# Routed experts of a transformer block: page row numbers copied out, an expert converted every third page, token sums kept by lanes, and the last two pages added on TensorE

## The reference

```
x = x + ln(attention(ln(x)))            # 16 heads of 16, RoPE, causal
t = ln(x)                               # 2048 x 256
combine = top-4 of softmax(t @ gate_w.T), 16 experts, renormalised
shared  = (silu(t@Wg) * (t@Wu)) @ Wd * sigmoid(t @ gate_vec)       # 704 wide
sparse  = sum over experts e of combine[:, e] * ((silu(t@Ge)*(t@Ue)) @ De)   # 176 wide
x = x + ln(shared + sparse)
```

## Time and profile before

| | |
|---|---|
| median of 3 executions | 587.03 us |
| lowest, highest | 582.26, 588.21 us |
| profiled execution, own time | 591.91 us |
| its span in the profile | 590.2 us |
| busy: TensorE, VectorE, ScalarE, GpSimd | 523.0, 412.6, 344.1, 317.2 us |
| page loop and what follows | from about 396 us to the end |

### The profile page before, as it was taken

One profiled execution on the slowest core, in us unless ns is written; L12 is line 12 of the kernel. 1 busy time (PEld: TensorE's weight loads), 2 busy tenths in 40 slices (PEclk: granted clock), 3 DMA queues, 4 the chain that ended last, 5 costly groups with the idle time before them and its releaser, 6 DMA issues.

```text
span 590.2 us, 11696 instructions
## 1 busy us (share of the span) xinstructions
PE 523.0 (89%) x3590; PEld 400.3 (68%) x3590; DVE 412.6 (70%) x1019; ACT 344.1 (58%) x704; POOL 317.2 (54%) x341
## 2 busy tenths in 40 slices
PE   8978889899999998879879887879989899999964
PEld 3744454656565453458668776769988899999953
DVE  4888878898788856688634552557977666566846
ACT  3443665686578558766443324547876766666633
POOL 4822724481465225222766656405758777778662
PEclk9988999999999999989899989799999999999987
DMA  8543560734073440520235412558999887788975
GB/s 310 159 120 116 186 205 4 217 113 140 27 222 109 141 142 3 170 83 2 85 131 184 165 72 98 185 160 200 223 209 235 146 138 133 129 146 174 280 174 204
DMA packets 71659, 87.66 MB, mean 149 GB/s; under 512 B 6640, under 2 KB 64560, under 8 KB 71600
## 3 DMA queue, kind: packets, MB, share of 16 engines
q1 hardware_dynamic: 56720, 67.22, 36.6%
q0 software_dynamic: 14448, 19.31, 18.0%
q10 hardware_dynamic: 432, 0.39, 0.2%
HBM read 34.99 MB, written 39.12 MB: 126 GB/s over the span
## 4 chain that ended last, share of the span: by engine, by line
PE 27%; DMA 7%; DVE 6%; issue 5%; another core or an unknown queue 4%; POOL 3%; ACT 3%; SPq 1%; POOLq 0%; ACTq 0%; DVEq 0%
PE gate_ps L2150 9%; PE y_ps L2173 5%; DMA acc_dram<-yout,xin 5%; PE y_ps L2124 2%; PE gate_ps L1092 2%; PE m_ps L2073 2%; PE up_ps L1092 2%; POOL acc_dram L1595 1%; DMA added<-acc_dram 1%; DVE hid_lo L1881 1%; PE up_ps L2161 1%; PE y_ps L2177 1%; DVE hid L1853 1%; PE up_ps L2162 1%
## 5 line engine op out<-in xcount | busy, mean ns | idle before, releaser
L1595 POOL DMA_INDIRECT acc_dram<-yout,xin x79 | 124.8, 1580 | 60.5 <-DMA acc_dram<-yout,xin 22.9
L815 DVE TENSOR_REDUCE nmax<-a_ps 128x2 f32<-128x768 f32 (+3 forms) x88 | 96.3, 1121 | 16.0 <-PE a_ps L983 15.5
L678 ACT ACTIVATE probs<-a_ps 128x1024 f32<-128x1024 f32 (+1 forms) x96 | 81.6, 883 | 30.9 <-PE a_ps L1008 26.3
L570 POOL TENSOR_SCALAR_AFFINE_SELECT probs<-probs 128x256 f32<-128x256 f32 (+1 forms) x96 | 47.2, 501 | 87.4 <-ACT probs L678 87.2
L1583 POOL DMA_INDIRECT xs_dram<-xrow,idx x64 | 66.5, 1040 | 37.3 <-issue 18.6
L2150 PE MATMUL gate_ps<-w_all,rxT_hi 128*128 x316 | 77.4, 327 | 3.8 <-DVE rxT_lo L1929 2.4
L1954 DVE TENSOR_TENSOR h<-rsilu,gate_ps 128x176 f32<-128x176 f32 x79 | 26.6, 336 | 45.1 <-ACT rsilu L1705 40.3
L2173 PE MATMUL y_ps<-w_all,hT_hi 128*128 x237 | 57.2, 310 | 1.0 <-DVE hT_lo L1966 0.7
L978 PE MATMUL a_ps<-KTt,QT 96*128 96x128 bf16 (+3 forms) x256 | 50.8, 309 | 5.7 <-ACT probs L678 1.8
L2150 PEld LDWEIGHTS gate_ps<-w_all,rxT_hi 128*128 128x128 f32 x316 | 51.8, 188 | 5.5 <-issue 5.0
L1008 PE MATMUL a_ps<-QT,KTt 99*128 99x512 bf16 (+3 forms) x256 | 47.9, 301 | 4.7 <-DVE nmax L815 1.7
(11 more groups left out here) (341 smaller groups left out, 1388.2 us busy)
## 6 DMA issues: line engine op xcount, KB each, us to landing
xin<-xs_dram SPq DMA_DIRECT2D x79, 136.5 KB
xs_dram<-zeros SPq DMA_DIRECT2D x7, 1365.0 KB, 6.5
w_all<-in_wex_dram SPq DMA_DIRECT2D x16, 480.0 KB
KTt<-parts SPq DMA_DIRECT2D x42, 128.0 KB
QT<-parts SPq DMA_DIRECT2D x39, 128.0 KB
acc_dram<-zeros SPq DMA_DIRECT2D x6, 640.0 KB, 7.7
ring<-acc_dram SPq DMA_DIRECT2D x18, 128.0 KB
acc_dram<-yst SPq DMA_DIRECT2D x4, 512.0 KB
```

The lines of the kernel that those rows point to most:

```text
L570: pool.affine_select(out=pr, in_=pr, pattern=[[0, nh], [1, P]], compare_op=ALU.is_ge, fill=0.0, base=0, channel_multiplier=-1).then_inc(ma ...
L678: nc.scalar.activation(dst, src, ACT.Exp, scale=float(DH) ** -0.5).then_inc(a_act, 1)
L815: nc.vector.tensor_reduce(nmax[:, i, h:h + nh].rearrange("p (b h) -> p b h", h=hb), src, AX.X, ALU.max, negate=True).then_inc(a_dve, 1)
L1595: pool.indirect_dma_start(out=acc[a][:, :], out_offset=bass.IndirectOffsetOnAxis(ap=xin[:, p % XIN, XROW - 1:XROW].bitcast(mybir.dt.uint32 ...
```

## The change

Four things are changed; the pages' computation is not.

- Row numbers: `select` copies the row numbers of its two pages out of `xin` into `row_of`, and the scatter takes them from there. A page load then waits until TensorE has turned the page that was in its slot and `select` has read it, no longer for that page's scatter.
- Experts: the conversion of an expert takes every third page instead of every second, in SyncE's order as in ScalarE's and VectorE's: an expert's transfers stand behind the loads of pages 16, 19, 22 and so on. The nine early tiles' loads stand behind all page loads.
- Lanes: `acc` has token row p * 16 + n instead of n * 128 + p (through the table `ids`), so a load of several tiles reads one contiguous run from each lane.
- The last two pages (77 and 78) are not scattered. VectorE builds for each a 128 x 512 matrix of ones and zeros: whether the row of the page (partition) belongs to the token of tiles 12 to 15 (column). TensorE multiplies with it (`spared`, 2 x 4 matmuls) ahead of the sums of tiles 12 to 15; their table comes with one more 256 KB transfer, `lanes`. The order of the three sums is now 2, 0, 1. (One semaphore of `gathered` is replaced by a common one.)

```diff
+SPARED = 2
+        def over_pages(q):
+            c = q % XIN
+            flat = xin[:, c:c + 2, :].rearrange("p a b -> p (a b)")
+            return flat[:, 0:TB * P]
+        lanes, owners = over_pages(67), [over_pages(69), over_pages(72)]
+        def by_lanes(rows):
+            return rows[0:NT * P, :].rearrange("(p n) d -> p n d", n=NT)
...
             def load_page(q):
                 if q >= XIN:
-                    sp.wait_ge(y_added[(q - XIN) % ACCS], 16 * ((q - XIN) // ACCS + 1))
+                    sp.wait_ge(r_turned, q - XIN + 1)
+                    sp.wait_ge(r_sel, (q - XIN) // 2 + 1)
...
-                    sp.dma_start(fetched(i, a), acc[a][i * P:(i + 1) * P, :]).then_inc(early_in[i % RING], 16)
+                    sp.dma_start(fetched(i, a), by_lanes(acc[a])[:, i, :]).then_inc(early_in[i % RING], 16)
...
                 load_page(q)
-                k = early + TAILS + (q - SPLIT - XIN) // 2
-                if q >= SPLIT + XIN and (q - SPLIT) % 2 == 0 and k < E:
+                k, part = divmod(q - SPLIT - XIN, 3)
+                k += early + TAILS
+                if k >= early + TAILS and part == 0 and k < E:
                     expert(k)
-                if FINAL + XIN <= q < FINAL + XIN + RING:
-                    load_early(q - FINAL - XIN)
+            for a in range(ACCS):
+                sp.wait_ge(y_added[a], 16 * len(range(a, FINAL + 1, ACCS)))
+            for i in range(RING):
+                load_early(i)
+            sp.wait_ge(r_turned, 69)
+            sp.wait_ge(r_sel, 35)
+            sp.dma_start(lanes, lanes_in).then_inc(lanes_in_sem, 16)
...
-            for a in (1, 2, 0):
-                sp.wait_ge(y_added[a], 16 * len(range(a, PAGES, ACCS)))
+            for a in (2, 0, 1):
+                sp.wait_ge(y_added[a], 16 * len(range(a, PAGES - SPARED, ACCS)))
                 load_rest(a, PARTS[1], total_in[a])
...
-            for p in range(PAGES):
+            for p in range(PAGES - SPARED):
...
-                        ap=xin[:, p % XIN, XROW - 1:XROW].bitcast(mybir.dt.uint32), axis=0),
+                        ap=row_of[:, p:p + 1].bitcast(mybir.dt.uint32), axis=0),
...
-                k = early + (p - SPLIT - 2) // 2
-                if p >= SPLIT + 2 and k < E:
-                    if (p - SPLIT) % 2 == 0:
+                k, part = divmod(p - SPLIT - 2, 3)
+                k += early
+                if early <= k < E:
+                    if part == 0:
                         expert_high(k)
-                    else:
+                    elif part == 1:
                         expert_tail_high(k)
...
+                nc.vector.tensor_copy(row_of[:, 2 * m:2 * m + n].bitcast(mybir.dt.int32),
+                                      xin[:, at:at + n, XROW - 1].bitcast(mybir.dt.int32))
...
+            def owns():
+                dve.wait_ge(lanes_in_sem, 16)
+                for k in range(SPARED):
+                    q = PAGES - SPARED + k
+                    ins = nc.vector.tensor_copy(named[:, k:k + 1], xin[:, q % XIN, XROW - 1:XROW].bitcast(mybir.dt.int32))
+                link(ins)
+                for k in range(SPARED):
+                    ins = nc.vector.tensor_scalar(owners[k], lanes, named[:, k:k + 1], None, ALU.is_equal)
+                ins.then_inc(owned, 1)
...
+            owns()
             gathered(0)
...
+            def spared():
+                pe.wait_ge(r_y, PAGES)
+                pe.wait_ge(owned, 1)
+                for k in range(SPARED):
+                    for i in range(PARTS[1].start, PARTS[1].stop):
+                        n = i - PARTS[1].start
+                        nc.tensor.matmul(pe_places[i], owners[k][:, n * P:(n + 1) * P],
+                                         yout[:, (PAGES - SPARED + k) % YOUT, :],
+                                         start=k == 0 and n % 2 == 0, stop=False, skip_group_check=True)
...
                 ins.then_inc(pe_summed, 1)
-            pe.wait_ge(r_y, PAGES)
-            for a in (1, 2, 0):
+                if i == 7:
+                    spared()
+            for a in (2, 0, 1):
                 pe.wait_ge(total_in[a], 16)
...
-    ids = np.arange((NT + 1) * P, dtype=np.int32).reshape(NT + 1, P).T
+    ids = np.concatenate([np.arange(NT * P).reshape(P, NT), NT * P + np.arange(P)[:, None]], axis=1)
```

More of the change, by code:

```diff
@@ L1256, in first_slots, with ffn_block @@
     yield
-def ffn_block(nc, t, wsh_in, wex_in, out):
+def ffn_block(nc, t, wsh_in, wex_in, lanes_in, out):
     with ExitStack() as ctx:
@@ L1480, in store_shared @@
                 b = ORDER_S[i]
-                sp.dma_start(acc[0][b * S:(b + 1) * S, :].rearrange("(n p) d -> p n d", p=P),
+                sp.dma_start(by_lanes(acc[0])[:, b * TB:(b + 1) * TB, :],
                              yst[:, i % 2]).then_inc(ysh_stored[i % 2], 16)
@@ L1535, in load_rest @@
                 to = added[:, a - 1] if a else total
-                sp.dma_start(to[:, tiles, :], acc[a][tiles.start * P:tiles.stop * P, :].rearrange(
-                    "(n p) d -> p n d", p=P)).then_inc(landed, 16)
+                sp.dma_start(to[:, tiles, :], by_lanes(acc[a])[:, tiles, :]).then_inc(landed, 16)
             for a in range(ACCS):
                 load_rest(a, slice(EARLY, PARTS[0].stop), rest_in)
-            for a in (1, 2, 0):
-                sp.wait_ge(y_added[a], 16 * len(range(a, PAGES, ACCS)))
+            for a in (2, 0, 1):
+                sp.wait_ge(y_added[a], 16 * len(range(a, PAGES - SPARED, ACCS)))
                 load_rest(a, PARTS[1], total_in[a])
@@ L1969, in _ @@
                     select(p // 2)
-                k = early + (p - SPLIT - 3) // 2
-                if p >= SPLIT + 3 and k < E:
-                    if (p - SPLIT) % 2 == 1:
+                k, part = divmod(p - SPLIT - 3, 3)
+                k += early
+                if early <= k < E:
+                    if part == 0:
                         expert_low(k)
-                    else:
+                    elif part == 1:
                         expert_tail_low(k)
@@ L2237, in build @@
         attention_block(nc, t, x, wqkv, wpair, wo, gw, rope, ids, wsh, cst, cst16)
-        ffn_block(nc, t, wsh, wex, out)
+        ffn_block(nc, t, wsh, wex, lanes, out)
 def kernel(L0_attn_x, L0_attn_Wq, L0_attn_Wk, L0_attn_Wv, L0_attn_Wo, L0_ffn_gate_w, L0_ffn_expert_gate_up,
```

26 lines of the change are left out of this document (15 added, 11 removed).

## The result

| | before | changed |
|---|---|---|
| median of 20 executions each | 588.62 us | 582.05 us |
| lowest, highest | 581.15, 594.43 us | 574.22, 590.86 us |
| ratio, with its 95% interval | | 0.9877 (0.9843 to 0.9910) |
| profiled execution, its span | 591.91, 590.2 us | 582.78, 581.0 us |

The change makes the kernel 1.2% faster, some 7.2 us. The three executions shown before had a median of 587.03 us; 0.9877 times that is 579.8 us, the time forecast. In another series on another chip the same kernel stood at 0.9912 (0.9881 to 0.9943), so the gain is about 0.9% to 1.2%; the medians of all executions stand at 0.9888 and 0.9875. The ratios leave out executions more than 1.5% above the fastest of their kernel, and the profiled execution of the kernel before is one of those.

A forecast was written before the change was run, and what follows sets the result against it. TensorE was taken to bound the calm page loop, with 8.7 us lost where experts are converted. From the median 587.03, 4.6 for the loop and 2.6 for the end gave 579.8 us; range 574 to 588.

The forecast's parts named there:

- The loop's mechanism: Page loop: ScalarE waits 7.8 us for expert transfers queued behind page loads that wait for scatters; freeing these removes it.
- transfers saturated: Rival, expert stretch: the transfers' engines, not queue order, make experts late; only the end gains, 584.4 us; chance 0.12.
- The loop's size: Page loop: 7.0 us saved in the profiled execution (bounds 0 to 8.7), 4.6 us taken for the median.
- pages 0 to 78 in 156 to 158 us: Sign that the forecast is right: the page loop shortened to this from 163.9 us.
- My check for VectorE: Page loop with experts every third page: VectorE needs 5.1 of 5.97 us in three pages, so it has room.
- its 2.6 for the end: Behind the last page: tile 11 done at 573.3 instead of 575.96 us; gain 2.6 us, bounds -2 to +3.
- Copies and `owns` at no cost: VectorE: 40 copies, at most 7.2 us busy, covered by room in the pages; `owns`, 1.9 us, hidden; cost 0.
- Early tiles at zero: Early tiles' loads in one burst behind page 62's landing: bounds -0.9 to +1.5 us, taken as 0.
- under 5: Sign that the forecast is right: loads of three tiles behind the loop take less than 5 us.
- it looks like the end's bound and hardly is: End: the last scatter and its `acc[0]` load seem to bound it, but VectorE waits only 0.22 us for the result.
- without the idle 4.93 us it should keep the full clock: End, TensorE: condition for the spared pages' matmuls costing 3.7 us; at the slow clock they cost 8.3 us.
- The slower rival: Page loop: scatters become the bound from a 6.3 us cycle of three on; 592.8 or 600.8 us; chance 0.12.

The follow-up runs named there:

- u1: Changed kernel with experts converted every second page again instead of every third; 0.9824 of the kernel before.
- e1: Kernel before with only row numbers copied, page loads freed from waiting for scatters, and early tiles' loads behind all page loads; 0.9946 of the kernel before.
- e2: Kernel before with only the conversion of experts moved to every third page; 0.9958 of the kernel before.
- b_again: The kernel before, unchanged, run and profiled a second time; 1.0032 of the kernel before, 0.9995 by the medians.
- u2: Changed kernel with page loads waiting for scatters again, experts still every third page; 1.0028 of the kernel before.
- u4: Changed kernel with the sums' rows back in the old layout by tiles; 0.9863 of the kernel before.
- e3: Kernel before with only the sums' row layout changed to lanes; 1.0026 of the kernel before, 0.9994 by the medians.
- u3: Changed kernel with all 79 pages scattered, none spared, and the last sums in the old order; 0.9947 of the kernel before.
- c_changed: The changed kernel itself, run again in a later series on another chip; 0.9912 of the kernel before.
- s_spared_alone: Kernel before with only the last two pages added by TensorE, plus the row-number copies this needs; 0.9994 of the kernel before, 0.9953 by the medians.
- v1: Changed kernel with experts every second page, measured a second time on another chip; 0.9922 of the kernel before.
- v2: Changed kernel with experts every second page and rows by tiles, leaving only freed page loads and spared pages; 0.9873 of the kernel before.

## Why the prediction was right, and where only its sum was

**The loop's mechanism: right.** ScalarE stood for experts whose fetch stood behind page loads that stood for scatters. With the page loads freed (u1, e1) that wait fell from 7.8 us to 0 and 0.2. The rival "transfers saturated" falls: the share rose to 0.98 and nobody waited. What I hadn't said: the change holds two cures for one wait. Either alone does it (e1: 161.9 us, e2: 160.1 us), and together they bring the loop to 159.4, within the spread of these numbers over kernels with freed loads (158.6 to 161.9 us).

**The loop's size: the term was too large for the profile, right for the median.** I took 7.0 us off the profiled execution and 4.6 off the median, between 2.1 and 7.0 for not knowing which part of the stalls the median execution had. The loop measured 4.5 us shorter in the first pair of profiles and 5.4 against b_again. So the sign "pages 0 to 78 in 156 to 158 us" was missed by 1.4. The other loss remained: 159.4 - 155.2 = 4.2 us, 2.7 of them between pages 6 and 38 and 1.4 from page 68 on. My check for VectorE was a mean, 5.1 of 5.97 us in three pages; on the one step where `select` and the low part meet, VectorE holds TensorE up all the same, but that is 0.5 us in all and the rest of the 2.7 is open. That the sum came out as 579.8 to the tenth is luck: its 4.6 is the middle between two readings of one long execution, its 2.6 for the end turned out 3.3 against one profile of before and nothing against the other, and by the later series it would be 587.03 x 0.9912 = 581.9 us.

**Copies and `owns` at no cost: right.** 40 copies took 8.7 us, 218 ns as the view counts them against the 181 taken; `owns` took 1.2 us, not 1.9; TensorE's spared matmuls 3.62 us for 16 records against 3.7, at full clock.

**Early tiles at zero: right here, by a condition that I didn't name.** u2 shows 8.3 us of standing once page loads wait for scatters. I had weighed the burst and not the place in the queue. e1's 3.0 us show that the cover is thin even with freed loads.

**The end: the number came out, its reasons didn't all.** Tile 11 was done at 567.1 us, 8.9 behind the loop's end, forecast 9.4, before 12.0. But in b_again, with the old kernel, it was done after 8.4 us: the 12.0 belonged to one long execution, and the chain through the load of tiles 9 to 11, from which I took the 2.6 us, is not what the change shortened. That load was there 6.8 us behind its issue, forecast 6.2, so not "under 5"; of the 2.5 us that I allowed for the layout nothing is shown (u4, e3), and b_again has the same end as the changed kernel.

The step "it looks like the end's bound and hardly is" was true of the kernel before and false of the kernel that the other parts make. In every kernel with a stall-free loop and all pages scattered (u3, e1, e2), VectorE stood 3.4 to 4.0 us for the last sum, and the end took 26.5 to 28.4 us. What the spared pages do is keep 2 to 5 us from being given back at the end (c_changed beside e1 and e2, u4 beside u3), and the rows show two halves of it: in u3, e1 and e2 the sums of tiles 12 to 15 start 1.8 to 3.1 us later than in b_again, and 16 of their records take 1.7 to 2.7 us longer, at the lower clock. With them, TensorE has matmuls in the stretch in which it otherwise stands, the first sum is asked for some 6 us sooner than in u3, and the clock stays up. I had named "without the idle 4.93 us it should keep the full clock" as a condition of the cost of 3.7 us; I didn't count it as a gain.

The two profiles of before go the same way: the short end, 22.95 us, is the one at 1.00, the long one, 26.3, the one at 0.58 (its tiles 9 to 11 also landed 2.2 us later). Whether the parts gain more together than singly isn't shown: e1 and s_spared_alone gained 0.5% and 0.1%, v1 and v2, which hold both parts, 0.8% and 1.3%; by the medians it is 0.7% and 0.5% against 1.25% and 1.3%, a plain sum.

**The slower rival: not seen.** It needed a scatter cycle of 6.3 us in the calm stretch. There it was 5.75 us (changed) and 6.10 (e3) against 6.11 (b_again 6.10), and beside experts 7.08 against 7.14. (Its 592.8 and 600.8 us were counted from 168.0 us for 79 pages; 79 x 163.9/78 is 166.0, so both should have been 2 us higher.) GpSimd took up to 2.36 us for a scatter beside the 1.15 us low part, as in the earlier trace rows. The Trainium skill, SBUF — State Buffer, section Who interferes with whom, says that a VectorE instruction with two SBUF inputs contends with a GpSimd instruction that reads SBUF; the low part has two such inputs, and the 2.36 us against 1.54 agree. The copies did not add to it: the 27 scatters that met a copy and no low part took 1.53 to 1.57 us but for one of 1.66, those that met neither 1.54 us in the median.

```profile
L1616 POOL DMA_INDIRECT acc_dram<-yout,row_of x77: 1532/1541/2362, 401.6 to 559.6; - x77
```

The Trainium skill, DMA: Bandwidth & Descriptors, section Latency and other measured facts, has slower copies for rows far apart by a large power of two; by 16 KB here e3 shows no effect.

**What stays open.** No run filled TensorE's idle time without also sparing a scatter and moving the loads of the sums, so how the 2 to 5 us divide between the clock and the earlier sums is read from rows of one profile each, not tried. Nor is it settled which idle stretches cost the clock: b_again idled 2.70 us ahead of tile 11 and kept it, e2 2.62 and lost it (the last two records of tile 11 took 1.06 us, in e1 0.59), and e1 lost it only behind its second wait. That the sums are late because the scatters are longer behind (the last starts 6.6 to 8.0 us behind the last once-a-page row in u3, e1 and e2, 5.8 to 6.3 in before, b_again and e3) was only argued. How often the old kernel's end is the short or the long one, two profiles don't say, and with it what the spared pages are worth alone. And whether experts every second page are better than every third: four ratios from 0.9824 to 0.9922 don't tell.

## What to carry to other kernels

A command at the head of a queue that waits makes everything behind it late; freeing it and giving the late ones more slack are two cures for one loss, and their gains aren't added. A step at the end is to be priced in the kernel that the other edits leave, not in the profile of before (here 0 to 2.5 us alone, and 2 to 5 us behind a faster loop), and by what it does to TensorE's clock, not only by its own work. And when a load is moved behind others in a queue, ask what those others wait for in the same change.

## What the runs showed that I had not expected

- A queue may stand for 101.8 us in all (e2) or 40.7 + 30.0 us (changed) within a loop of 160 us without costing anything; 81.0 us of the same kind of wait cost 7.8 us of ScalarE's time in the kernel before. The total says nothing; what the waiting command holds back does.
- The load of three tiles out of the three sums takes 6.4 to 7.6 us from its first issue in 3 KB runs and 6.4 to 8.8 us in 1 KB runs, while scatters and other loads are under way; the runs' length can't be told from the spread. The 2.6 us of the output's stores were no lower bound that such a load comes near to.
- A wait of TensorE near the end can be paid twice: the same 16 records took 3.69 us at a granted clock of 1.00 (b_again) and 6.02 to 6.43 us at 0.50 (u3, e2), and in the same kernel the clock behind such a wait was 0.58 in one execution and 1.00 in another. 3.62 us of additional matmuls put into the wait cost nothing that can be measured (end 22.9 us in s_spared_alone and in b_again), and the clock stood at 1.00 in all eight profiles that had them.
